# A fused Mamba and expert layer: the B products read from SBUF, a fourth decay bank, the first norm's statistics on ScalarE, and another order at both ends

## The reference, cut to what matters

```
u  = silu(conv4(ctx @ in_proj) + conv_b)             # 1024 channels e, time t
dt = softplus(dt_proj(x_proj(u)) + dt_b); B, C = rest of x_proj(u)   # 16 states
state = state * exp(dt * A) + (dt * u) * B           # for every t, channel and state
y  = sum_over_states(state * C) + D * u
x  = x + tanh(g_xattn) * y * silu(layernorm(x))      # "first norm"
S  = softmax(layernorm(x) @ router_w + router_b)     # 16 experts
for each expert: the 256 tokens with the highest S
x  = x + tanh(g_ffn) * sum(S chosen) * (layernorm(x) @ expert_w + expert_b)
```

## Time and profile before

| | us |
|---|---|
| median of 3 runs (2107.14 to 2107.42) | 2107.32 |
| the profiled execution | 2105.8 |
| its span, first to last instruction | 2103.7 |
| busy in the span: VectorE / GpSimd | 1921.0 / 1759.3 |
| busy in the span: TensorE / ScalarE | 1648.5 / 1405.7 |
| first B product of VectorE starts | 65.8 |
| last scan ends | 1901.0 |

### The profile page before, as it was taken

The page is one execution under the profiler, slowest core; times in us unless marked ns, Lnnn a source line. Parts: engine busy times, 40 slices in busy tenths (PEclk is TensorE's granted clock), DMA queues, the critical chain, the costliest instruction groups (busy, mean ns, idle before and its releaser), DMA issues.

```text
span 2103.7 us, 23390 instructions
## 1 busy us (share of the span) xinstructions
PE 1648.5 (78%) x7572; PEld 1075.5 (51%) x7572; DVE 1921.0 (91%) x2044; ACT 1405.7 (67%) x2115; POOL 1759.3 (84%) x768
## 2 busy tenths in 40 slices
PE   7556666668988888889888998888888877778792
PEld 2234445545555555555555555555555555556341
DVE  7998989999999899999999899999999999993667
ACT  3455756777788767886788777886888677863000
POOL 0487999999999999998999999998999999995100
PEclk9678888889999999999999998999999989898896
DMA  9610214133743456353735374355634373337079
GB/s 366 250 35 17 86 52 181 41 116 107 287 154 104 165 193 224 116 182 126 281 115 178 112 283 158 96 166 191 232 111 160 132 268 113 127 102 297 20 287 391
DMA packets 139001, 348.19 MB, mean 166 GB/s; under 512 B 15234, under 2 KB 17794, under 8 KB 129666
## 3 DMA queue, kind: packets, MB, share of 16 engines
q1 hardware_dynamic: 138882, 346.71, 47.2%
HBM read 301.04 MB, written 45.61 MB: 165 GB/s over the span
## 4 chain that ended last, share of the span: by engine, by line
POOL 27%; PE 24%; DVE 18%; issue 16%; ACT 10%; DMA 5%; SPq 0%; DVEq 0%; POOLq 0%; ACTq 0%
POOL states L1371 16%; DVE states L1113 10%; POOL states L1359 9%; PE pY L615 7%; PE pM L709 4%; PE pA L583 4%; ACT pDec L877 3%; PE pA L592 2%; DVE states L1098 2%; DVE u L1088 2%; ACT L861 1%; PE pY L611 1%; POOL dtub L1350 1%; DMA bbc<-bc_scratch 1%; ACT L1036 1%
## 5 line engine op out<-in xcount | busy, mean ns | idle before, releaser
L1371 POOL TENSOR_TENSOR states<-states,cbc 128x2048 f32<-128x2048 f32 x256 | 1160.2, 4535 | 32.4 <-DVE states L1113 22.0
L877 ACT ACTIVATE pDec<-steps,an 128x512 f32<-128x512 f32 x1024 | 684.8, 687 | 409.5 <-DVE states L1113 404.9
L615 PE MATMUL pY<-con,states 128*128 128x128 f32 x4096 | 585.2, 305 | 187.5 <-POOL states L1371 187.3
L615 PEld LDWEIGHTS pY<-con,states 128*128 128x128 f32 x4096 | 540.0, 159 | 306.7 <-POOL states L1371 246.4
L1113 DVE TENSOR_TENSOR_SCAN states<-pDec,carry,states 128x512 f32<-128x512 f32 x512 | 625.7, 1265 | 23.4 <-ACT pDec L877 22.9
L1113 DVE TENSOR_TENSOR_SCAN states<-pDec,states 128x512 f32<-128x512 f32 x512 | 594.7, 1203 | 37.9 <-ACT pDec L877 37.7
L1359 POOL TENSOR_TENSOR states<-dtub,bbc 128x1024 f32<-128x1024 f32 x192 | 454.3, 2366 | 62.2 <-PE pY L615 50.5
L709 PE MATMUL pM<-wk,xfT 128*128 128x512 f32 x832 | 422.2, 623 | 0.0
L1098 DVE TENSOR_TENSOR states<-pU,bbc 128x1024 f32<-128x1024 f32 x320 | 384.9, 1203 | 5.0 <-DMA bbc<-bc_scratch 3.2
L583 PE MATMUL pA<-ctx_sb,winb 128*128 128x512 f32 x448 | 230.2, 662 | 62.9 <-issue 31.1
L709 PEld LDWEIGHTS pM<-wk,xfT 128*128 128x128 f32 x832 | 146.9, 202 | 80.2 <-issue 78.8
(11 more groups left out here) (211 smaller groups left out, 1425.3 us busy)
## 6 DMA issues: line engine op xcount, KB each, us to landing
wk<-in_expert_w SPq DMA_DIRECT2D x416, 256.0 KB, 4.4
bbc<-bc_scratch SPq DMA_DIRECT2D x32, 1024.0 KB, 7.3
cbc<-bc_scratch SPq DMA_DIRECT2D x32, 1024.0 KB, 9.4
sz<-in_x SPq DMA_DIRECT2D x34, 512.0 KB, 6.1
xt<-in_x SPq DMA_DIRECT2D x15, 1024.0 KB, 5.9
winb<-in_winT SPq DMA_DIRECT2D x58, 256.0 KB, 2.7
x_scratch<-xt SPq DMA_DIRECT2D x14, 1024.0 KB, 6.0
xr<-x_scratch SPq DMA_DIRECT2D x28, 512.0 KB, 4.1
```

What stands on the lines that cost most here:

```text
L615: mm = pe.matmul(pY[:, eT(t)], states[g % NST][:, i, eT(t)], ident, start=False, stop=(q == QG - 1 and i == QN - 1 and t == TT - 1), is_tr ...
L877: nc.scalar.activation(pDec[bank_of(h, k)][:], dt[e % 2], ACT.Exp, scale=an[:, k:k + 1]).then_inc(s_dec, 1)
L1371: nc.gpsimd.tensor_tensor(st, st, cbc[:, QW * q:QW * (q + 1), :], ALU.mult).then_inc(s_hc, 1)
```

## The change

VectorE's B products read `dtu` in SBUF, and wait for GpSimd's `dtu` instead of ScalarE's copy; the copy is gone. The bank joins the ring of decays (NDB 4). The first norm's statistics are made by VectorE for the first sequence only (4 pairs of tiles, in other places); those of the other three are made by ScalarE, 48 row tasks in slots 8 to 66 (the last in the second half), with a sum and a sum of squares per tile, loaded in pairs by SyncE. B and C are loaded as soon as they are in DRAM. The first context tile comes in four DMAs behind the first weights, and the head's constants, taps and statistics stand in another order. At the end VectorE makes the last C product in two parts, SLOTTED is 3 (8 matmuls move from the loop to the tail), and turns, norms and product steps stand in another order. Cut to its core:

```diff
-NDB = 3
+NDB = 4
-DCP_SLOT = [GQ * e - 2 for e in range(E)]
+NROWS = (B - 1) * E // 2
+ROW_SLOT = [8 + 5 * (i // 4) + i % 4 for i in range(4 * NROWS)]
+LN1_SLOT = ROW_SLOT[-1] + 2
-EARLY = 2
-SLOTTED = 4
+EARLY = [0, 2, 5, 8]
+SLOTTED = 3
...
-        pU = bank("pU")
...
-        stage = [x for t in (bbc, *pairs, cbc, sz) for x in tiles_of(t)]
-        stage += tiles_of(xt) + [xr[0][:], xr[1][:]] + tiles_of(wk)
+        places = [[xr[0][:], xr[1][:]], tiles_of(wk)[:2]]
+        stage = [*tiles_of(xt), *places[0], *places[1], *tiles_of(pairs[3])]
+        stage += [x for i in range(NROWS) for x in places[i % 2]]
...
+            def load_rows(i):
+                if i < 2:
+                    sp.wait_ge(s_ln1, 2 * (i + 2))
+                else:
+                    sp.wait_ge(s_rows, 5 * (i - 1))
+                load_stage(E // 2 + i)
...
-            load_ctx(0)
             sp.dma_start(win_first[0], winT[0]).then_inc(s_wf[0], 16)
+            for part in range(KC):
+                sp.dma_start(ctx_sb[:, part, :], ctxT[0, :, part, :]).then_inc(s_cf[part] if part < KC - 1 else s_ctx, 16)
...
             store_bc(0)
-            sp.wait_ge(s_ln1, 2 * STAGED_B)
-            for q in range(3):
-                load_b(0, q)
-            sp.wait_ge(s_ln1, 2 * STAGED_C)
-            for q in range(2):
-                load_c(0, q)
+            load_b(0, 0)
+            load_b(0, 1)
+            load_c(0, 0)
+            load_b(0, 2)
+            load_c(0, 1)
...
             def sum_states(h, g):
-                wait(pe, s_hc, n(h, NP, g // 2 + 1))
+                if h == LAST and g // 2 == NP - 1:
+                    pe.wait_ge(s_hcv, QN)
+                else:
+                    wait(pe, s_hc, n(h, NP, g // 2 + 1))
...
-            logits_end(LATE, 2)
             turn_end(LATE, 6)
             turn_end(LATE, 7)
+            logits_end(LATE, 2)
...
-            def dtu_copy(h, e):
-                wait(act, s_dt, n(h, E, e + 1))
-                wait(act, s_bmd, n_made(DVE_GROUPS, h, QG * e - 1))
-                nc.scalar.copy(pU[:], dtu[e % 2][:]).then_inc(s_dcp, 1)
...
+            def row_task(i):
+                pair, task = divmod(i, 4)
+                t = task % 2
+                k = 2 * pair + t
+                tile = places[pair % 2][t]
+                b, e = divmod(E + k, E)
+                if task == 0:
+                    act.wait_ge(s_stage[E // 2 + pair], 16 * 2)
+                if i:
+                    act.wait_ge(s_rows, 5 * pair + (0, 1, 3, 4)[task])
+                if task < 2:
+                    nc.scalar.activation(unread[:], tile, ACT.Copy, accum_out=sums1[:, t:t + 1]).then_inc(s_rows, 1)
+                if task == 1:
+                    act.wait_ge(s_rows, 5 * pair + 2)
+                    nc.scalar.activation(nm1[:, b, e - 1:e + 1], sums1, ACT.Copy, scale=-1.0 / D).then_inc(s_rows, 1)
+                if task >= 2:
+                    nc.scalar.activation(unread[:], tile, ACT.Square, bias=nm1[:, b, e:e + 1],
+                                         accum_out=sq1[:, b, e:e + 1]).then_inc(s_rows, 1)
...
             def times_b(h, g):
                 e, q = divmod(g, QG)
-                wait(dve, s_dcp, n(h, E, e + 1))
+                wait(dve, s_dt, n(h, E, e + 1))
...
-                nc.vector.tensor_tensor(states[g % NST], spread(pU), bbc[:, QN * q:QN * (q + 1), :], ALU.mult) \
+                nc.vector.tensor_tensor(states[g % NST], spread(dtu[e % 2]), bbc[:, QN * q:QN * (q + 1), :], ALU.mult) \
                     .then_inc(s_bmd, 1)
...
+            dve.wait_ge(s_cq[NQ - 1], n(LAST, 16, 16))
+            dve.wait_ge(s_scan, n(NC, NU, 0))
+            for i in range(QN):
+                st = pairs[(NP - 1) % (NST // 2)][:, QN * i:QN * (i + 1), :]
+                nc.vector.tensor_tensor(st, st, cbc[:, QW * (NQ - 1) + QN * i:QW * (NQ - 1) + QN * (i + 1), :],
+                                        ALU.mult).then_inc(s_hcv, 1)
             half(NC, REST)
...
             def step_times_u(h, e):
-                wait(pool, s_dcp, n(h, E, e - 1))
+                wait(pool, s_bmd, n_made(DVE_GROUPS, h, QG * (e - 1) - 1))
...
                 for i, k in at(CM_SLOT, g, h):
-                    times_c(k, i)
+                    if k * NP + i < NC * NP - 1:
+                        times_c(k, i)
```

More of the change, by code:

```diff
@@ L235, in mamba_moe @@
         s_c = sem("constants_ready")
+        s_cf = [sem(f"context_first{i}_in") for i in range(KC - 1)]
         s_ctx = sem("context_in")
@@ L460, in side @@
             def side(h, g):
+                if h == 0 and g == 0:
+                    load_rows(0)
+                    load_rows(1)
+                for i, k in at(ROW_SLOT, g, h):
+                    if k == 0 and i % 4 == 3 and i // 4 + 2 < NROWS:
+                        load_rows(i // 4 + 2)
                 for i, k in at(WIN_SLOT, g, h):
@@ L555, in _ @@
                 load_back(i)
+            store_unit(LATE, SLOTTED)
             for i in range(NC * TT):
@@ L811, in _ @@
             mm.then_inc(s_srt, 1)
-            first = EARLY * (TT - 1)
+            first = EARLY[-1]
             for i in range(BITS):
@@ L919, in xfT_out @@
                 wait(act, s_xfp, n(h, 2 * TT, f + 1))
+                if h == LATE and f == 5:
+                    act.wait_ge(s_y, n(LAST, E, E - 1))
+                    nc.scalar.copy(szT[1][:], pD[:]).then_inc(s_xfT, 1)
+                    return
                 p = n(h, 2 * TT, f)
@@ L992, in late @@
                     gate_out(k, e)
+                for i, k in at(ROW_SLOT, g, h):
+                    if k == 0:
+                        row_task(i)
                 for f, k in at(XFT_SLOT, g, h):
@@ L1142, in ln1_stats, with ln1_variance, ln1_bias @@
                     k = 2 * i + t
-                    z = nc.vector.bn_aggr(mv1[:, k // E, k % E, :], stats[i % 2][:, t, :, :].rearrange("p a s -> p (a s)"))
+                    z = nc.vector.bn_aggr(mv1[:, k, :], stats[i % 2][:, t, :, :].rearrange("p a s -> p (a s)"))
                 z.then_inc(s_ln1, 1)
-            def ln1_variance(rows, pairs):
-                dve.wait_ge(s_ln1, 2 * pairs)
-                nc.vector.tensor_scalar(ve1[:, rows, :], mv1[:, rows, :, 1], EPS, None, ALU.add).then_inc(s_ln1v, 1)
-            def ln1_bias(rows, k):
-                dve.wait_ge(s_rs1, k)
-                nc.vector.scalar_tensor_tensor(out=ln1[:, rows, 1, :], in0=mv1[:, rows, :, 0], scalar=-1.0,
-                                               in1=ln1[:, rows, 0, :], op0=ALU.mult, op1=ALU.mult).then_inc(s_ln1b, 1)
-                dve.wait_ge(s_ln1b, k)
+            def ln1_variance(k):
+                if k:
+                    dve.wait_ge(s_rows, 5 * NROWS)
+                    nc.vector.tensor_scalar(ve1[:, 1:B, :], sq1[:, 1:B, :], 1.0 / D, EPS, ALU.mult, ALU.add).then_inc(s_ln1v, 1)
+                else:
+                    dve.wait_ge(s_ln1, E)
+                    nc.vector.tensor_scalar(ve1[:, 0, :], mv1[:, :, 1], EPS, None, ALU.add).then_inc(s_ln1v, 1)
+            def ln1_bias(k):
+                dve.wait_ge(s_rs1, k + 1)
+                if k:
+                    z = nc.vector.tensor_tensor(ln1[:, 1:B, 1, :], nm1[:, 1:B, :], ln1[:, 1:B, 0, :], ALU.mult)
+                else:
+                    z = nc.vector.scalar_tensor_tensor(out=ln1[:, 0, 1, :], in0=mv1[:, :, 0], scalar=-1.0, in1=ln1[:, 0, 0, :],
+                                                       op0=ALU.mult, op1=ALU.mult)
+                z.then_inc(s_ln1b, 1)
+                dve.wait_ge(s_ln1b, k + 1)
             def ln2_stats(h, t):
@@ L1220, in _, with conv_first @@
             dve.wait_ge(s_w, 16 * NW)
+            def conv_first(j):
+                for i in range(HALO):
+                    conv(0, j, i, pIn[j])
+            conv_first(0)
             dve.wait_ge(s_c, 3)
```

111 lines of the change are left out of this document (54 added, 57 removed).

## The result

The changed kernel takes 2486.47 us (median of 4 runs, 2485.76 to 2488.33), the kernel before 2107.23 (4 runs, 2106.49 to 2107.42). The ratio is 1.180, with a 95% interval of 1.178 to 1.182. The forecast was 2502, in a range of 2355 to 2620. The profiled span is 2483.6 us.

A forecast was written before the change was run, and what follows sets the result against it. It took two nearly full engines, VectorE and GpSimd, to bound the loop. Head 51.5, 64 blocks of 35.15 and tail 197 gave 2498 us of span; execution and median offsets of 2.1 and 1.5 made 2502, range 2355 to 2620.

The forecast's parts named there:

- The mechanism: VectorE's B product, both inputs in SBUF, waits out the GpSimd instruction begun before it, then enters; mean about 2.7 us.
- no such wait: Rival, 8%: VectorE's streaming B products run as before beside GpSimd, so the change is a gain, 2036 us.
- GpSimd goes first: Rival, 7%: at each boundary GpSimd's queued instructions precede the waiting VectorE; 39.7 us a block, 2793 us.
- The walk through a block: B products' waits in the scan loop: 7.0 us per odd-half block, 8.5 per even; mean block 35.15 us.
- the half costs 8 blocks like the others: First half: its extra statistics, small operations and late loads go, leaving some 281 us like other halves.
- The gaps rival: Rival, 14%: B products nearly always fall due between GpSimd instructions; shared time bounds at 33.0 us a block, 2364 us.
- Decays' waits: VectorE's waits for ScalarE's decays in the loop, 0.8 us a block before, counted as gone.
- GpSimd's `dtu` and VectorE's products: GpSimd's step-size product waits for VectorE's products of the block before last; long fulfilled, 0 us.
- ScalarE's row tasks: 24 tiles of statistics, 62 us on ScalarE over the first 281 us: hidden, 0; at most 25 us without cover.
- Head and tail: First B product at 51.5 us, 14.3 earlier (10 to 18); tail after the last scan 197 us, 6 less.
- The product's own work: VectorE's B product alone, with both inputs in SBUF: 0.02 us more each, 0.1 per block.
- The sum: Whole kernel: 51.5 + 64 x 35.15 + 197 = 2498 us of span, 2502 us as time; forecast 70%.

The follow-up runs named there:

- e1: The changed kernel with VectorE's B products reading the PSUM copy again, made by ScalarE, and a ring of three decays: 2090.43 us.
- e2: The kernel before with only VectorE's B products reading the step-size product in SBUF, without ScalarE's copy: 2516.54 us.
- e4: The changed kernel with each of GpSimd's C products (128x2048) as two instructions of 128x1024: 2399.12 us.
- e9: The changed kernel with each of VectorE's B products as two instructions of 128x512: 2845.93 us.
- e5: The changed kernel with GpSimd's C products replaced by memsets of the same tile, which read nothing: 2128.01 us in one run.
- e11: The kernel before with three projections of the second half of the row moved, and all eight projections' taps put two slots behind them instead of three: 2089.14 us.
- e12: The changed kernel with the same move of projections and taps as in e11: 2456.82 us.
- e3: The changed kernel with decays in three PSUM banks only, the fourth idle: 2497.09 us.
- e8: The kernel of e1 with ScalarE's row statistics over 16 columns instead of 1024: 2083.2 us.

## Why the prediction was right, point by point

- **The mechanism.** VectorE stands until the GpSimd instruction that began first is over, and goes in at the next boundary. Shown: by e1 and e2 (one operand), e4 and e9 (boundaries, both directions) and e5 (a GpSimd instruction that only writes doesn't block). The rivals "no such wait" and "GpSimd goes first" fall with them: a product would take 1.2, or more than 7 where C and B are queued; the longest is 5.46.
- **The walk through a block.** Forecast for slots 1, 2, 4, 5, 7: waits of 0.9, 0, 0.5, 4.0 and 1.6 us. The block at 1001.8 begins at slot 4; in the order 4, 5, 7, 1, 2 it has 0.3, 3.7, 2.1, 0.8 and 0, forecast 0.5, 4.0, 1.6, 0.9 and 0. Same pattern, total 6.9 against 7.0. Blocks of halves 1 to 7 take 34.4 us on average (forecast 35.15): 0.7 too long by 56 blocks is 41 us. The mis-sized term is the even half: I gave it 35.4, it has 34.3 (the odd ones 34.5, forecast 34.9). GpSimd's carry copies there do go with longer waits, but less than I gave them: 7.4 to 7.7 us a block in halves 2, 4 and 6 (forecast 8.5), 6.7 in halves 1, 3 and 5 (forecast 7.0). The mean wait is 2.643 - 1.207 = 1.44 us a product in these halves, forecast 1.55.
- **The step that failed: "the half costs 8 blocks like the others".** Forecast 281, measured 303.5. I had put the whole excess of the first half before (258.6 against 225) down to statistics and late loads, and never asked TensorE's waits in that window. Moving the projections and their taps takes 17.4 us off the first half of the kernel before (e11) and 28.7 off that of the changed one (e12), whose excess over the others was 28. So in the changed kernel the excess came with the gate turns behind the projections' taps, which the change leaves where they are; in the kernel before, the same edit gave back 17 us of an excess of 32. The 22 us too few here hid behind the 41 too many in the other halves; the sum was closer than its terms.
- **The gaps rival** (2364). Its floor, 33.0 a block, came true in none of the seven later halves; the shortest had 33.9. The floor itself charges GpSimd the full 1.13 us of a product, where 0.9 to 1.0 were measured. That the slot lists set the phase at which the engines meet is my reading; no run moved them.
- **Decays' waits.** Forecast gone; 11.5 us left. e3: it is VectorE's standing more than the fourth bank.
- **GpSimd's `dtu` and VectorE's products.** Forecast "long fulfilled: 0". The profile has this wait seven times, 54.0 us in all, once shortly before each later half (e2, with the old order, has 54.1). There the first `dtu` of a half waits for all of VectorE's products of the half before, and not for those of the block before last. VectorE waits nowhere for GpSimd's B products; whether the waits cost anything by moving GpSimd's later instructions was not tried.
- **ScalarE's row tasks.** Forecast 0, upper bound 25. e8: about 6 us on e1, in the presence of the gate turns' waits; in e12, where those are gone, no excess is left for them.
- **Head and tail.** 51.5 against 51.10; 197 against 198.8. The gate product of the last half comes 5.8 us behind the last scan instead of 9.8, which is 4 of the 5 forecast.
- **The product's own work.** Forecast 0.02 us more with both inputs in SBUF. No such difference shows: the 43 products of the changed kernel that began beside no GpSimd instruction have a mean of 1.20 us, those of e1 1.21.
- **The sum.** 51.1 + 3.1 (to the first scan) + 303.5 + 1927.1 (seven halves) + 198.8 = 2483.6.

## What to carry to other kernels

Before an operand moves from PSUM to SBUF on VectorE, count the SBUF inputs of the instruction and look at what GpSimd does beside it: a second SBUF input cost 396 us here, with the instruction's own work unchanged at 1.2 us. If it must be so, shorten GpSimd's instructions (e4 gave back 87 us) and never VectorE's (e9 cost 359 more). And when one stretch of a periodic loop is longer than its siblings, read the waits of every engine in that stretch, those that are not the bound first of all: waits of 5 to 12 us on TensorE, at 71 to 78% busy, led to an edit that was worth 17 to 30 us.

## What the runs showed of the hardware that I had not expected

- The waiting engine goes in at the very next boundary, in both directions. Splitting the shorter side's instruction is harmful: halves of 657 ns take up to 5.04 us (e9).
- The two sides pay alike. Each is longer by what was left of the other's instruction, less some 0.13 us: 3.70 of 3.83 us for VectorE, 0.98 of 1.12 and 0.90 of 1.04 for GpSimd. GpSimd pays less only because a VectorE product is short.
- With GpSimd out of the way, the product with both inputs in SBUF takes 1.19 to 1.22 us (43 products of the changed kernel), that with one in PSUM 1.20 to 1.23 (e1) or 1.17 to 1.23 (before). By itself, the place of the operand makes no difference that shows here.
